# A transformer block on one core: the output projection done as three split products, its sums transposed back

## Chip, cores and metric

The kernel runs on 1 core of one Trainium2 chip. The metric is the device time in microseconds. Before the change the median of 3 runs is 757.2 us (757.11 to 757.91).

## What is computed

16 sequences of 256 rows with 128 features go through attention and a mixture of experts. Cut to what matters here:

```python
x = L0_attn_x                                   # (16, 256, 128)
xn = layernorm(x)
q, k, v = per head (16 heads of 64): xn @ Wq[h], xn @ Wk[h], xn @ Wv[h]
attn = softmax(causal(q @ k.T / 8))
heads = concat over h of attn @ v               # (256, 1024) for each sequence
y = xn + heads @ Wo                             # Wo: (1024, 128)
x1 = x + layernorm(layernorm(y, 1e-3) * gamma + beta)
# router: top 2 of 8 experts for each row, gelu(row @ w1[e]) @ w2[e], gated sum
out = x1 + layernorm(experts(layernorm(x1)))
```

The change concerns `heads @ Wo` and what reads its result.

## The kernel before

The five engines run programs of their own, written out by hand in order, and meet at semaphores. The attention is a loop over 16 batches (one sequence each, two tiles of 128 rows), each of `STEPS` = 4 steps; a step takes two pairs of heads. Below, step 1 to step 4 stand for u = 0 to 3. Several batches are under way at once: while batch b is in the steps, batch b-1 has its output sums normalised and batch b-2 goes through the router. After the 16 batches, 39 tiles of 256 rows go through the experts (lines 691 to 725), and at the end the two results of each row are summed and normalised.

One step on PE (line 480): the projection of one pair's q and k, `product3` twice (lines 384 to 395, six products of 256 columns on operands of type F32R, high and low parts; the low by low product is left out); the transposes of an earlier pair's probabilities (`p_transpose`, lines 439 to 448, the late rows into bank PT1O first); `w_o` for one pair (line 431); the second pair's projection, `p_transpose` and `w_o`; a third of the values' projection (`v_proj`, line 397); attention times values for two pairs (`pv_two`, line 427, into PT1O); the scores of the next two pairs and their masks (lines 402 to 416).

`w_o` takes the head sums `hT` (features on the partitions, in plain F32) as the stationary operand and `wo_sb` as the moving one, once for each of the two row tiles, and adds up over the 8 pairs in bank A:

```python
last = mm(A[:, t * D:(t + 1) * D], hT[:, par, t * P:(t + 1) * P], wo_sb[:, c, :], ...)
```

The result has the rows on the partitions. `hT` is made by one ACT copy out of PT1O at each step (`o_copy`, line 1278), which counts `o_sb`; PE waits on `o_sb` before it writes PT1O again with `p_transpose`, and before `w_o`.

One step on DVE (line 811): the maxima of the first pair's scores (lines 777 and 778); the copy of the late transposes `pT1` (line 794); `normalise_pair` of an earlier pair (lines 784, 786, 788), whose end, `nrm`, PE's second `p_transpose` waits for; the maxima of the second pair, again the copy and, behind some work of other batches, `normalise_pair`. The work of other batches has fixed places. For batch b-1 these are: `attended` (line 1042, adds `xn` to bank A) and `attention_stats` in step 2, `first_norm` (z1) and `second_stats` in step 3, `finish` (z3) in step 4. POOL makes the inverse roots between them, `z2 = z1 * gamma + beta` after `first_norm`, and `x1` after `finish`. For batch b-2, parts 0 to 6 of `router` are spread over the steps, with `dispatch` of batch b-3 at the end of step 1.

One step on ACT (line 1313): the copies of q and k, the exponentials, the copies of the transposes, `v_copy` (line 1273) out of bank M, and `o_copy`. In step 2 PE transposes the next batch's rows into bank M (`x_transpose`, line 375), for which it waits for `v_copy`, and only then come the scores.

After the last batch, `last_pairs` and `last_sums` (lines 578 to 605 for PE, 891 for DVE) finish the attention between the first products of the experts.

## Time and profile before

| | |
|---|---|
| median of 3 runs | 757.2 us |
| profiled execution, its own time | 757.12 us |
| its span on the core | 755.3 us |
| mean granted TensorE clock | 0.981 of full speed |
| busy share of the span | PE 93%, weight load 79%, DVE 75%, ACT 69%, POOL 37% |
| chain that ended last, by engine | PE 51%, DVE 24%, ACT 14%, POOL 2%, DMA 2%, issue and the queues the rest |
| the part before the experts | from 0 to some 570 us |

A busy time counts an instruction from start to end, and neighbours overlap: a matmul that the profile gives 0.28 us may be followed by the next after 0.12 us. What an instruction takes of its engine is the distance to the next start, and it is this that the chain of waits shows. A busy share is a mean over stretches that have different limits.

### The profile page before, as it was taken

The numbers are of one execution on the slowest core, as the hardware profiler recorded it, in microseconds if no ns is written. First come the engines' busy times: TensorE is split into PE (matmuls) and PEld (weight loads), VectorE is DVE, ScalarE is ACT, GpSimd is POOL, SyncE is SP. The second block draws the span as 40 slices with busy tenths as digits, with TensorE's granted clock in tenths as the row PEclk, the third lists the DMA queues.
The fourth block names the chain that finished last, engine by engine and source line by source line (L and its number), as shares of the span: only waits on it lengthen the run. The fifth ranks groups of instructions, "written<-read, shape, count | busy, mean of one in ns | idle before, by whom it ended". The sixth has DMA issues, their size and how long they took to land.

```text
span 755.3 us, 17697 instructions
## 1 busy us (share of the span) xinstructions
PE 700.0 (93%) x5954; PEld 596.4 (79%) x5955; DVE 564.9 (75%) x1914; ACT 524.5 (69%) x1687; POOL 277.5 (37%) x388
## 2 busy tenths in 40 slices
PE   4899999999999999999999999999989897999954
PEld 3688877788888888888888888888879797999921
DVE  5568888889897988888797988888896673444216
ACT  4776877877787777887787778887774563555505
POOL 3022534232323233232323232232314676655535
PEclk9999999999999999999999999999999998999978
DMA  8620000000000000000000000000020233222155
GB/s 184 205 40 8 9 8 16 17 27 10 23 8 23 8 23 16 17 23 15 22 8 23 8 23 13 19 23 9 16 66 30 73 111 97 76 78 79 45 175 173
DMA packets 43701, 34.88 MB, mean 46 GB/s; under 512 B 10624, under 2 KB 40320, under 8 KB 43616
## 3 DMA queue, kind: packets, MB, share of 16 engines
q1 hardware_dynamic: 37984, 23.81, 12.0%
q0 software_dynamic: 4544, 9.45, 3.5%
q8 instruction: 47, 0.77, 0.4%
q10 hardware_dynamic: 1088, 0.54, 0.3%
q14 instruction: 38, 0.31, 0.1%
HBM read 20.22 MB, written 13.56 MB: 45 GB/s over the span
## 4 chain that ended last, share of the span: by engine, by line
PE 51%; DVE 24%; ACT 14%; issue 4%; DMA 2%; DVEq 2%; POOL 2%; SPq 0%; POOLq 0%; ACTq 0%
PE M L684 8%; PE SC L406 6%; PE PT1O L423 6%; DVE prob L786 5%; ACT prob L1266 4%; PE SC L414 3%; DVE prob L788 3%; ACT prob L1260 3%; PE M L385 3%; DVE nmax L778 3%; PE PT1O L442 3%; PE SC L409 3%; ACT qk L1255 3%; PE M L387 2%; PE M L386 2%
## 5 line engine op out<-in xcount | busy, mean ns | idle before, releaser
L1255 ACT ACTIVATE qk<-M 128x512 f32<-128x512 f32 x127 | 76.1, 599 | 96.2 <-PE M L387 96.2
L1266 ACT ACTIVATE prob<-SC,nmax 128x256 f32<-128x256 f32 x256 | 123.5, 482 | 0.0
L423 PE MATMUL PT1O<-pT,v_sb 128*64 128x256 f32 (+1 forms) x1024 | 97.7, 333 | 0.7 <-ACT pT L1271 0.7
L423 PEld LDWEIGHTS PT1O<-pT,v_sb 128*64 128x64 f32 x1024 | 63.6, 137 | 42.5 <-issue 21.7
L1536 POOL DMA_INDIRECT expert_rows<-v_sb,got x78 | 77.1, 989 | 52.1 <-ACT v_sb L1410 33.9
L1260 ACT ACTIVATE prob<-SC,nmax 128x128 f32<-128x128 f32 x256 | 93.3, 370 | 3.6 <-DVE nmax L778 3.6
L786 DVE TENSOR_TENSOR prob<-prob,rden 128x512 f32<-128x512 f32 x128 | 90.1, 704 | 4.5 <-DVE rden L784 0.2
L1525 POOL DMA_INDIRECT sent_rows<-rec,slot x64 | 67.1, 1049 | 56.9 <-DVE slot L1030 37.9
L778 DVE TENSOR_REDUCE nmax<-SC 128x2 f32<-128x512 f32 x128 | 87.1, 680 | 0.0
L385 PE MATMUL M<-xt_hi,wqk_hi 128*128 128x256 f32 x254 | 82.6, 325 | 3.3 <-DVE xt_lo L772 2.4
L406 PE MATMUL SC<-qk 64*128 64x256 f32 x512 | 83.6, 403 | 0.6 <-ACT prob L1266 0.6
L777 DVE TENSOR_REDUCE nmax<-SC 128x2 f32<-128x256 f32 x128 | 53.4, 417 | 38.2 <-PE SC L414 38.0
L1271 ACT ACTIVATE pT<-PT 128x512 f32<-128x512 f32 x128 | 76.3, 596 | 3.8 <-PE PT L447 3.0
L684 PE MATMUL M<-w_sb,hidT 128*128 x624 | 78.0, 279 | 0.9 <-ACT v_sb L1410 0.9
L434 PE MATMUL A<-wo_sb,hT 128*128 128x128 f32 x512 | 78.2, 276 | 0.0
L684 PEld LDWEIGHTS M<-w_sb,hidT 128*128 128x128 f32 x624 | 74.5, 196 | 1.2 <-issue 1.1
L387 PE MATMUL M<-xt_hi,wqk_lo 128*128 128x256 f32 x254 | 72.0, 283 | 0.0
L386 PE MATMUL M<-xt_lo,wqk_hi 128*128 128x256 f32 x254 | 71.9, 283 | 0.0
L434 PEld LDWEIGHTS A<-wo_sb,hT 128*128 128x128 f32 x512 | 67.5, 193 | 0.0
L1410 ACT ACTIVATE v_sb<-M,got 128x128 f32<-128x128 f32 x78 | 24.4, 363 | 57.1 <-PE M L684 55.6
L442 PE MATMUL PT1O<-ident,prob 128*128 128x128 f32 x256 | 52.8, 288 | 11.3 <-DVE prob L788 8.0
L447 PE MATMUL PT<-ident,prob 128*128 128x128 f32 x256 | 63.2, 274 | 0.0
(186 smaller groups left out, 1789.3 us busy)
## 6 DMA issues: line engine op xcount, KB each, us to landing
got<-sent_rows SPq DMA_DIRECT2D x39, 132.0 KB, 2.3
w_in<-expert_rows SPq DMA_DIRECT2D x16, 256.0 KB, 3.6
x_in<-L_attn_x SPq DMA_DIRECT2D x16, 128.0 KB, 2.1
w_in<-L_ffn_w SPq DMA_DIRECT2D x1, 2048.0 KB, 12.0
x_res<-L_attn_x SPq DMA_DIRECT2D x16, 128.0 KB, 2.1
w_sb<-L_ffn_w SPq DMA_DIRECT2D x8, 256.0 KB, 4.4
out<-y_out SPq DMA_DIRECT2D x8, 256.0 KB, 2.1
sent_rows<-pad_rec SPq DMA_DIRECT2D x11, 132.0 KB, 4.2
```

Source lines behind the costliest of these rows:

```text
L385: mm(dst, a_hi, b_hi, start=start, stop=False, skip_group_check=True)
L386: mm(dst, a_hi, b_lo, start=False, stop=False, skip_group_check=True)
L387: return mm(dst, a_lo, b_hi, start=False, stop=True, skip_group_check=True)
L406: mm(SC[par][:, k, LATE_Q], qk[r, par, 0, P:S], qk[r, par, 1, :], start=True, stop=False, skip_group_check=True)
L423: last = mm(PT1O[k * E:(k + 1) * E, cols], v_sb[:, t, h * E:(h + 1) * E], src[:, par, k, :], start=(t == 0), stop=(t == 1), skip_group_che ...
L434: last = mm(A[:, t * D:(t + 1) * D], hT[:, par, t * P:(t + 1) * P], wo_sb[:, c, :], start=(c == 0 and t == 0), stop=(c == NP - 1), skip_gr ...
L684: last = mm(out_bank[:, t * D:(t + 1) * D], hidT[:, s, c, t * P:(t + 1) * P], w2_e[:, c * D:(c + 1) * D], start=(t == 0 and c == 0), stop= ...
L778: v.tensor_reduce(nmax[:, par, 0, :], SC[par][:, :, LATE_Q], AX_X, ALU.max, negate=True).then_inc(mx, 1)
L786: v.tensor_tensor(prob[:, slot, :, 1:3, :], prob[:, slot, :, 1:3, :], rden[:, par, 0, :].unsqueeze(2).unsqueeze(3).broadcast_to([P, 2, 2, ...
L1255: a.activation(qk[:, p % 2], src[:].rearrange("p (i s) -> p i s", i=2), ACT.Copy).then_inc(qk_sb, 1)
L1260: return a.activation(prob[:, slot, k, 0, :], SC[par][:, k, EARLY_Q], ACT.Exp, bias=nmax[:, par, 1, k:k + 1], accum_out=den[:, par, 1, k:k ...
L1266: return a.activation(prob[:, slot, k, 1:3, :].rearrange("p n t -> p (n t)"), SC[par][:, k, LATE_Q], ACT.Exp, bias=nmax[:, par, 0, k:k + 1 ...
```

## The change

- The output weights are split at the start into `wo_hi` and `wo_lo` (POOL, two instructions of 1024 columns behind `pad_ids(0)`), and PE's first `w_o` waits for them.
- `o_copy` writes `hT_hi` (type F32R), and DVE makes `hT_lo` = PT1O - `hT_hi` in a new instruction `o_low`, 128x512, at the start of every step, in front of the maxima. It is now `o_low` that counts `o_sb`.
- `w_o` is one `product3` for a pair: three products of 256 columns, weights stationary, head sums moving. Bank A holds the sums transposed.
- In step 2 ACT copies them to `att_t` (`sums_copy`, in front of `v_copy`), and PE transposes them back into bank A (`sums_transpose`, in front of `x_transpose`).
- `attended` reads them from there and moves from step 2 to the start of step 3. `attention_stats` moves from the end of step 2 to the middle of step 3, `first_norm` from the middle of step 3 to its end, `second_stats` from the end of step 3 to the middle of step 4, `finish` from the middle of step 4 to its end. `xn` gets a third buffer for this.
- To make room, `hidT`, the experts' hidden rows, shares the memory of `wqk_in`, and `y_out` that of `prob`.

```diff
-        xn = [sb(f"xn{n}", [P, T, D]) for n in range(2)]
+        xn = [sb(f"xn{n}", [P, T, D]) for n in range(3)]
...
             def w_o(c):
                 par = c % 2
-                for t in range(T):
-                    last = mm(A[:, t * D:(t + 1) * D], hT[:, par, t * P:(t + 1) * P], wo_sb[:, c, :],
-                              start=(c == 0 and t == 0), stop=(c == NP - 1), skip_group_check=True)
+                last = product3(A[:, 0:S], wo_hi[:, c, :], wo_lo[:, c, :], hT_hi[:, par, :], hT_lo[:, par, :],
+                                start=(c == 0))
...
+            def sums_transpose(b):
+
+                pe.wait_ge(sem("att_t"), b + 1)
+                for t in range(T):
+                    last = nc.tensor.transpose(A[:, t * D:(t + 1) * D], att_t[:, t * P:(t + 1) * P], ident[:])
+                last.then_inc(sem("sums_mm"), 1)
...
+                if k == 2:
+                    pe.wait_ge(sem("wo_ok"), 1)
...
+                if u == 1 and there(b, 1):
+                    sums_transpose(b - 1)
...
             def in_front_of_down(n):
+                if n == 1:
+                    sums_transpose(B - 1)
...
+            def o_low(k):
+                dve.wait_ge(sem("o_hi"), k)
+                v.tensor_tensor(hT_lo[:].rearrange("c n (t p) -> c n t p", t=T),
+                                PT1O[:].rearrange("c (n p t) -> c n t p", n=2, t=T),
+                                hT_hi[:].bitcast(F32).rearrange("c n (t p) -> c n t p", t=T), ALU.subtract).then_inc(o_sb, 1)
...
+                if u == 2 and there(b, 1):
+                    attended(b - 1)
+                if k >= 2:
+                    o_low(k - 1)
                 maxima(p)
...
                 if u == 1:
-                    if there(b, 1):
-                        attended(b - 1)
...
                 if u == 2:
                     if there(b, 1):
-                        first_norm(b - 1)
+                        attention_stats(b - 1)
...
                 if u == 3:
                     if there(b, 1):
-                        finish(b - 1)
+                        second_stats(b - 1)
...
-                if u == 1:
-                    if there(b, 1):
-                        attention_stats(b - 1)
                 if u == 2:
...
                     if there(b, 1):
-                        second_stats(b - 1)
+                        first_norm(b - 1)
                 if u == 3:
                     if there(b, -2):
                         x_stats(b + 2)
+                    if there(b, 1):
+                        finish(b - 1)
...
                 expert_weights(1, w1_at[1])
                 split_rows(1, 1, M[:, ROWS:2 * ROWS])
+                o_low(STEPS * B - 1)
                 normalise_pair(end - 1)
                 pT1_copy(end - 2)
...
                 pT1_copy(end - 1)
+                o_low(STEPS * B)
...
             def o_copy(k):
                 act.wait_ge(pv_mm, k)
-                a.activation(hT[:].rearrange("c n (t p) -> c n t p", t=T), PT1O[:].rearrange("c (n p t) -> c n t p", n=2, t=T),
-                             ACT.Copy).then_inc(o_sb, 1)
+                a.activation(hT_hi[:].rearrange("c n (t p) -> c n t p", t=T), PT1O[:].rearrange("c (n p t) -> c n t p", n=2, t=T),
+                             ACT.Copy).then_inc(sem("o_hi"), 1)
+
+            def sums_copy(b):
+                act.wait_ge(sem("wo_mm"), b + 1)
+                if there(b, 1) and there(b, -1):
+                    act.wait_ge(sem("lg_done"), b)
+                a.activation(att_t[:], A[:, 0:S], ACT.Copy).then_inc(sem("att_t"), 1)
...
+                if u == 1 and there(b, 1):
+                    sums_copy(b - 1)
                 turn = v_turn(b, u)
...
+            pool.wait_ge(sem("wo_ld"), 16)
+            q.tensor_copy(wo_hi[:], wo_sb[:]).then_inc(sem("wo_h"), 1)
+            pool.wait_ge(sem("wo_h"), 1)
+            q.tensor_tensor(wo_lo[:], wo_sb[:], wo_hi[:].bitcast(F32), ALU.subtract).then_inc(sem("wo_ok"), 1)
```

Line numbers of the changed kernel differ from those before: its maxima are lines 795 and 796, its `normalise_pair` 802 to 806, its normalisations 773.

The first place is DVE at the seam of steps 3 and 4 in a steady batch, from the last part of `normalise_pair` to the next maxima. Before:

```order
L788 TENSOR_TENSOR prob<-prob,rden 128x2x128
L770 CAST xt_hi<-xt_st 128x256 [waits xt_st,v_mm]
L772 TENSOR_TENSOR xt_lo<-xt_st,xt_hi 128x256 [waits xt_h]
L745 BN_STATS stat_z<-z 128x6 [waits z2_done]
L745 BN_STATS stat_z<-z 128x6
L750 BN_AGGR mv_z<-stat_z 128x2 x2
L777 TENSOR_REDUCE nmax<-SC 128x2 [waits s_mm]
L778 TENSOR_REDUCE nmax<-SC 128x2
```

Now:

```order
L806 TENSOR_TENSOR prob<-prob,rden 128x2x128
L788 CAST xt_hi<-xt_st 128x256 [waits xt_st,v_mm]
L790 TENSOR_TENSOR xt_lo<-xt_st,xt_hi 128x256 [waits xt_h]
L773 TENSOR_SCALAR z<-att,mv_a,rstd_a 128x128 [waits rstd_a]
L773 TENSOR_SCALAR z<-att,mv_a,rstd_a 128x128
L831 TENSOR_TENSOR hT_lo<-PT1O,hT_hi 128x512 [waits o_hi]
L795 TENSOR_REDUCE nmax<-SC 128x2 [waits s_mm]
L796 TENSOR_REDUCE nmax<-SC 128x2
```

The statistics of z are gone from here, the normalisation to z1 (two instructions) is here in their place, and in front of the maxima stands the new subtraction with its wait on `o_hi`.

The second place is DVE in the middle of step 4, behind the second maxima and the copy `pT1`. Before:

```order
L778 TENSOR_REDUCE nmax<-SC 128x2
L794 COPY pT<-PT1O 128x256 [waits t1_mm]
L755 TENSOR_SCALAR z<-z,mv_z,rstd_z 128x128 [waits rstd_z]
L755 TENSOR_SCALAR z<-z,mv_z,rstd_z 128x128
L1003 CAST topf<-topi 128x16
L1006 TENSOR_TENSOR sel<-iota_e,topf 128x16 x2
L1008 TENSOR_TENSOR sel_bf<-sel 128x16
```

Now:

```order
L796 TENSOR_REDUCE nmax<-SC 128x2
L812 COPY pT<-PT1O 128x256 [waits t1_mm]
L763 BN_STATS stat_z<-z 128x6 [waits z2_done]
L763 BN_STATS stat_z<-z 128x6
L768 BN_AGGR mv_z<-stat_z 128x2 x2
L1032 CAST topf<-topi 128x16
L1035 TENSOR_TENSOR sel<-iota_e,topf 128x16 x2
L1037 TENSOR_TENSOR sel_bf<-sel 128x16
```

The two instructions that made z3 have left for the end of the step, and the statistics of z stand here.

The third place is PE at the end of step 2, between `pv_two` and the scores. Before:

```order
L423 MATMUL PT1O<-pT,v_sb 64x256 x2
L423 MATMUL PT1O<-pT,v_sb 64x128 x2
L378 MATMUL M<-ident,xn 128x128 [waits xn_done,v_done]
L378 MATMUL M<-ident,xn 128x128
L406 MATMUL SC<-qk 128x256 [waits exp_done,qk_sb]
```

Now:

```order
L429 MATMUL PT1O<-pT,v_sb 64x256 x2
L429 MATMUL PT1O<-pT,v_sb 64x128 x2
L448 MATMUL A<-ident,att_t 128x128 [waits att_t]
L448 MATMUL A<-ident,att_t 128x128
L384 MATMUL M<-ident,xn 128x128 [waits xn_done,v_done]
L384 MATMUL M<-ident,xn 128x128
L412 MATMUL SC<-qk 128x256 [waits exp_done,qk_sb]
```

Two transposes that wait for ACT's copy `att_t` have come in front of those of the next batch's rows.

## Rows read from the trace of the kernel before

**Rows 1.** Windows, one steady batch: busy us (x) of PE, PEld, DVE, ACT, POOL; PEclk; DMA

```profile
305.00:339.00 34.00, 33.51 (x301) 28.05 (x297) 29.38 (x103) 26.79 (x94) 10.61 (x15) 1.00 0.06 17
```

**Rows 2.** Chain of waits, two steps in the middle: start us, us, engine, tile, line

```profile
305.24 0.44 PE M L378 x2
...
324.85 0.23 PE PT1O L442 x2
...
326.34 0.35 DVE prob L788
...
326.73 0.44 PE PT1O L442 x2
...
327.61 0.45 PE A L434 x4
...
331.92 0.54 PE SC L414 x4
...
332.68 0.12 PE M L385
...
333.43 0.60 ACT qk L1255
...
338.79 0.49 ACT v_sb L1275
...
339.33 0.44 PE M L378 x2
```

**Rows 3.** Timeline of DVE, same stretch: start, us, what, [idle before <-releaser]

```profile
322.82 0.48 DVE L745 BATCH_NORM_STATS2 stat_x<-x_in 128x6 f32<-128x128 f32 x2
...
323.54 0.14 DVE L1014 COPY rec<-top 128x2 f32<-128x2 f32 x1
...
323.95 0.42 DVE L777 TENSOR_REDUCE nmax<-SC 128x2 f32<-128x256 f32 x1
...
325.10 0.43 DVE L794 COPY pT<-PT1O 128x256 f32<-128x256 f32 x1
...
326.59 0.42 DVE L777 TENSOR_REDUCE nmax<-SC 128x2 f32<-128x256 f32 x1
...
327.52 0.42 DVE L794 COPY pT<-PT1O 128x256 f32<-128x256 f32 x1
...
331.90 0.17 DVE L1030 CAST slot<-slot_f 128x4 int32<-128x4 f32 x1
332.28 0.42 DVE L777 TENSOR_REDUCE nmax<-SC 128x2 f32<-128x256 f32 x1 [0.21 <-PE SC L414]
...
333.69 0.42 DVE L794 COPY pT<-PT1O 128x256 f32<-128x256 f32 x1 [0.39 <-PE PT1O L442]
```

**Rows 4.** Line 1180 on DVE, durations in ns: min/median/max, first and last start

```profile
L1180 DVE TENSOR_TENSOR wv_hi<-PT,wv_hi x37: 424/425/425, 571.8 to 711.3; 128x256 fp32r<-128x256 f32 x37
```

**Rows 5.** Timeline of ACT, end of the second step of a batch

```profile
305.77 0.41 ACT L1250 ACTIVATE xt_st<-M 128x256 f32<-128x256 f32 x1
306.06 0.20 ACT L1289 ACTIVATE ex<-lg 128x16 f32<-128x16 f32 x1
```

**Rows 6.** Lines 994 and 1003 on DVE as in Rows 4; POOL timeline

```profile
L994 DVE TENSOR_TENSOR pr<-ex,rrs x16: 174/448/454, 105.0 to 609.7; 128x16 f32<-128x16 f32 x16
L1003 DVE CAST topf<-topi x16: 175/750/753, 114.3 to 611.7; 128x16 f32<-128x16 uint32 x16
320.41 0.73 POOL L1512 TENSOR_TENSOR x<-x_res,z 128x256 f32<-128x256 f32 x1 [3.18 <-DVE z L755]
```

**Rows 7.** Timelines of PE and DVE, behind the last step of attention

```profile
564.77 1.05 PE L434 MATMUL A<-wo_sb,hT 128*128 128x128 f32 x8
...
564.92 0.17 DVE L784 RECIPROCAL rden<-den 128x4 f32<-128x4 f32 x1
```

**Rows 8.** Timeline of PE, first batch; chain of waits near 560 us

```profile
30.05 0.44 PE L378 MATMUL M<-ident,xn 128*128 128x128 f32 x2 [0.92 <-ACT v_sb L1275]
...
559.77 0.85 PE A L434 x4
```

More of the change, by code:

```diff
@@ L80, in sandwich_kernel @@
         wo_sb = sb("wo_sb", [P, NP, D])
+        wo_hi = sb("wo_hi", [P, NP, D], F32R)
+        wo_lo = sb("wo_lo", [P, NP, D], F32R)
         w1_in = sb("w1_in", [P, NE, F])
@@ L111, in sandwich_kernel @@
         pT1 = sb("pT1", [P, 2, 2, P])
-        hT = sb("hT", [P, 2, S])
+        hT_hi = sb("hT_hi", [P, 2, S], F32R)
+        hT_lo = sb("hT_lo", [P, 2, S], F32R)
+        att_t = sb("att_t", [P, S])
         shift = sb("shift", [P, 2, GT])
@@ L177, in sandwich_kernel @@
         w1_e = wqk_hi[:].rearrange("p i c -> p (i c)").rearrange("p (s i f) -> p s i f", s=2, i=2)
-        hidT = sb("hidT", [P, 2, NF, ROWS])
+        hidT = wqk_in[:].rearrange("p i c -> p (i c)").rearrange("p (s c r) -> p s c r", s=2, c=NF)
         yo = v_sb[:].rearrange("p t c -> p (t c)")[:, 0:RING * ROWS].rearrange("p (k t d) -> p k t d", k=RING, t=2)
@@ L183, in sandwich_kernel @@
         zn = hidT[:, 0].rearrange("p c r -> p (c r)").rearrange("p (s k d) -> p s k d", s=2, k=GT)
-        y_out = sb("y_out", [P, 2, GT, D])
+        y_out = prob[:].rearrange("p s k n t -> p (s k n t)")[:, 0:2 * GT * D].rearrange("p (s k d) -> p s k d", s=2, k=GT)
         SC = [ctx.enter_context(nc.psum_tensor(f"SC{n}", [P, 2, 512], F32)) for n in range(2)]
@@ L377, in x_transpose @@
                 for t in range(T):
-                    last = nc.tensor.transpose(M[:, t * P:(t + 1) * P], xn[b % 2][:, t, :], ident[:])
+                    last = nc.tensor.transpose(M[:, t * P:(t + 1) * P], xn[b % 3][:, t, :], ident[:])
                 last.then_inc(sem("xt_mm"), 1)
@@ L477, in _ @@
             pe.wait_ge(sem("wv_ok"), 1)
-            pe.wait_ge(sem("wo_ld"), 16)
             def step(b, u):
@@ L809, in _ @@
             v.tensor_tensor(wv_lo[:], wv_in[:], wv_hi[:].bitcast(F32), ALU.subtract).then_inc(sem("wv_ok"), 1)
+            def o_low(k):
[3 more added lines that the diff above has]
+                                hT_hi[:].bitcast(F32).rearrange("c n (t p) -> c n t p", t=T), ALU.subtract).then_inc(o_sb, 1)
             def step(b, u):
-                p = 2 * (STEPS * b + u)
+                k = STEPS * b + u
+                p = 2 * k
                 first = p == 0
+                if u == 2 and there(b, 1):
+                    attended(b - 1)
+                if k >= 2:
+                    o_low(k - 1)
                 maxima(p)
@@ L1037, in x_normalise @@
                 dve.wait_ge(sem("rstd_x"), b + 1)
-                if b >= 2:
-                    dve.wait_ge(sem("att_done"), b - 1)
-                normalise("x", xn[b % 2], x_in, T).then_inc(sem("xn_done"), 1)
+                if b >= 3:
+                    dve.wait_ge(sem("att_done"), b - 2)
+                normalise("x", xn[b % 3], x_in, T).then_inc(sem("xn_done"), 1)
             def attended(b):
-                dve.wait_ge(sem("wo_mm"), b + 1)
+                dve.wait_ge(sem("sums_mm"), b + 1)
                 if there(b, 1) and there(b, -1):
                     dve.wait_ge(sem("logit_mm"), b)
-                v.tensor_tensor(att[:], xn[b % 2][:], A[:, 0:T * D].rearrange("p (t d) -> p t d", t=T), ALU.add)\
+                v.tensor_tensor(att[:], xn[b % 3][:], A[:, 0:T * D].rearrange("p (t d) -> p t d", t=T), ALU.add)\
                     .then_inc(sem("att_done"), 1)
@@ L1428, in _ @@
                     gated(n, k, it)
+                    if n == 0:
+                        sums_copy(B - 1)
             with act.Fori(EARLY // RING, TILES // RING) as it:
```

## The prediction

> **What bounds the kernel now.** I read the windows first, then the chain of waits over one batch, then the timelines of DVE, ACT and PE over the same stretch. A batch takes 34.09 us, from one transposing of the next rows to the following (305.24 to 339.33 [rows 2]). In a steady batch PE is busy 33.5 of 34 us and DVE 29.4 [rows 1], so PE looks like the bound and DVE like an engine with 4.6 us to spare. The chain says something narrower. In steps 1 and 4 it passes from PE's late transposes (324.85 [rows 2]) to DVE's copy `pT1` (325.10 [rows 3]), over the normalisation (its end at 326.34 + 0.35) back to PE (326.73), and stays on PE until the masks (331.92) [rows 2]. In step 2 it runs on ACT without a gap from the copy of q and k (333.43) to `v_copy` (338.79), and PE's transposes of the next rows wait for that (339.33) [rows 2]. In step 3 it runs mostly on DVE. What decides is thus not how much DVE idles but where. At the seam of steps 4 and 1 the maxima start at 323.95 with no idle in front of them. A pair of maxima takes 0.93 us (326.59 to 327.52), so they end at 324.88, and the copy behind them starts at 325.10: 0.22 us of room. At the seam of 1 and 2 there is 0.21 us of idle in front of the maxima (332.28), which end at 333.21, and the copy starts at 333.69: 0.48 more [rows 3]. From 3 to 4 there is none. The rest of DVE's idle time lies in step 2, while ACT works.
>
> **What PE gains.** A `w_o` takes 0.45 us before, one F32R product of 256 columns 0.12 [rows 2], so three of them 0.36: 0.09 less, for 128 calls 11.5 us. The two transposes back take 0.23 (as the pair at 324.85 [rows 2]), 16 times 3.7. PE's own work falls by 7.8 us. Little of it reaches the end: the first `w_o` of a step is done while DVE normalises, the second is on the chain in steps 1 and 4 only, and there DVE will be later than PE.
>
> **What ACT adds.** `sums_copy` is a copy of 128x256 out of PSUM. The one of the same size at 305.77 is followed at 306.06 [rows 5]: 0.29 us. It stands in front of `v_copy` in step 2, where ACT is the chain, so it counts in full. The transposes back on PE fall into the wait for `v_copy`.
>
> **What DVE adds.** `o_low`, 128x512, PSUM minus SBUF, has no equal in the trace. The nearest is line 1180, half its size, 424 ns [rows 4]; its distance to the next start is about 0.34. The pair of maxima reads 768 elements of PSUM in 0.93 us [rows 3], which for 512 makes 0.62. I take 0.62; the ends are 0.34 and 0.69 (the time that the normalisation takes for its 512 elements).
>
> By the Trainium skill (VectorE: DVE Perf Modes, the errata section), a DVE instruction that reads PSUM takes 120 cycles more than its elements at 0.96 GHz, an estimate of 0.66 us here; the sum would be 1.6 us higher.
>
> DVE's order is the second half of the matter. `attended` and `attention_stats` leave step 2, where DVE has time. `attended` is at the start of step 3 still in that time. `attention_stats` is not: it takes the place of `first_norm`, that of `second_stats`, that of `finish`, and `finish` goes to the end of step 4. So the stretch from the first maxima of step 3 to the first copy `pT1` of the next step 2 holds one set of statistics more, 0.72 us (322.82 to 323.54 [rows 3]), and three `o_low`. The fourth, in front of step 3's maxima, waits only for ACT's copy, which is there before the masks: free.
>
> Walk along that stretch: it is DVE alone, work after work, once the room is used up. Added: 3 x 0.62 + 0.72 = 2.58 us. Room used up: 0.22 + 0.21 + 0.48 = 0.91 [rows 3]. That leaves 1.67, and with ACT's 0.29 a batch takes 1.96 us more.
>
> Against that stands a relief. Line 994 takes 448 ns in the loop and 174 at least, line 1003 750 and 175 [rows 6]. Line 994 runs while POOL makes z2, and line 1003 starts together with POOL's x1 at 320.41 [rows 6]: the two engines get in each other's way on SBUF operands. Line 1180, with one operand in PSUM, never varies (424 to 425 ns [rows 4]). In the changed order z2 falls under `o_low` and the maxima, which read PSUM, so line 994 gets back 0.27 us. x1 moves away from line 1003, which gets back up to 0.57, but now starts beside the small copies of `router` part 6; I take half, 0.28. So a batch costs 1.96 - 0.55 = 1.41 us.
>
> The stretch is full from batch 2's step 3 (the router's parts are there from then on) to batch 15's step 2: 13 times, 18.3 us. In batches 0 and 1 DVE has room, PE's 0.09 in some steps and ACT's 0.29 once cancel: 0.
>
> **The end of the attention.** In batch 15 step 2 has PE on the chain, so 0.23 - 0.09 = 0.14. `o_low` in front of step 4's maxima, less the relief of line 994: 0.35. In `last_pairs` PE reaches the double `w_o` at 564.77, while DVE begins its normalisation at 564.92 [rows 7]; the new `o_low` stands in front of that normalisation and PE now waits for it. That is 0.62 for `o_low` itself, the 0.15 between the two starts, and about as much again as `o_low` (an estimate) for `finish`, which has moved in front of it: 1.4 us, less 0.18 for the faster `w_o`. Together 1.7 us. `sums_transpose` in front of the second tile and the last `o_low` have the first tile's stores beside them: nothing. The split of the weights on POOL lies in the first step, where POOL idles, and PE's first `w_o` comes in the third: nothing; if it were late, that `w_o` would wait a few us once. The shared memory of `hidT` and `y_out` moves no instruction.
>
> **Sum.** 18.3 + 0 + 1.7 = 20.0 us on the profiled execution's 757.12, which is 0.1 below the median of the runs: 777 us.
>
> **Rivals.**
> *PE sets the time (faster).* If DVE had 0.62 us of room at each seam, PE's 7.8 us less would show: 749 us. For it speaks PE's busy share, 33.5 of 34 [rows 1]. Against it: the maxima at 323.95 have no idle in front of them and 0.22 behind [rows 3]. It decides if an `o_low` takes under about 0.25 us. Chance 0.04.
> *Only ACT's copy counts.* If the moved statistics and the subtractions find room after all (router parts cheaper in the new order), 15 x 0.29 less some of PE's gain and plus the 1.7 us of the end: 761 us. Against it again the seam without idle. Chance 0.07.
> *POOL and DVE collide more.* After the change POOL's two instructions for z2 begin as DVE passes into step 4, its inverse root runs beside line 1006, and x1 beside part 6 of the router. If no relief comes and one more instruction is held for as long as line 1003 is (0.57), a batch takes 1.96 + 0.3 to 0.57: 757 + 13 x 2.4 + 2 = 790 us. Chance 0.13.
> By the Trainium skill (SBUF: State Buffer, the section on the two separate sides), the pair of ports that DVE and GpSimd share goes whole to whichever starts first, for all of its instruction, and a DVE instruction contends if it has two SBUF inputs or runs in a two-port mode; by this rule the router's copies would lose the full length of x1, which is this rival. The durations of lines 994 and 1003 agree with it.
> *The clock falls.* PE now waits about 2 us more in each batch. A TensorE at half clock takes 0.85 us for a `w_o` at 559.77, against 0.45 [rows 2, 8]. If that came once a batch for some 4 us, 13 x 2 = 26 more: 803 us. Against it: the waits are split over three steps, and after one of 0.92 us in the first batch the transposes still take their 0.44 us [rows 2, 8], as at 339.33. The granted clock in the window is 1.00 [rows 1]. Chance 0.05.
>
> **How the numbers follow.** My forecast has 0.71. Its own bounds: `o_low` at 0.34 makes 39 x 0.28 = 11 less, 766; at 0.69, no relief, 777 + 3 + 7 = 787. The range 766 to 789 takes in nearly all of the forecast and the smaller half of the collisions; left out are 749, 761, 803 and the top of the collisions, some 0.2. A change of 0.2%, 1.5 us, is about what a measurement of this kernel can tell from none. Faster 0.04, same 0.02 (a lower case of the second rival), slower 0.94.
>
> **What would show it.** In the profile after: `o_low` 64 times with a mean near 0.69 us busy; DVE without idle from step 3 to step 2, its idle time gathered in front of the maxima of step 3; PE waiting for `nrm` or `o_sb` in steps 4 and 1, up to 0.7 us each; the batches 35.5 us long, where they were 34.09; the product in F32R at 0.12 us for each of three; the clock at 1.00. Wrong would be: idle time on DVE at the seams of steps 3, 4 and 1; PE's `w_o` products further apart than 0.12; a batch under 34.5 us.

## The result, and the profile after

| | before | after |
|---|---|---|
| median of 4 runs each | 757.33 us | 779.3 us (777.88 to 780.77) |
| ratio after to before, 95% interval | | 1.0296 (1.0271 to 1.0321) |
| profiled execution, its own time | 757.12 us | 780.77 us |
| its span on the core | 755.3 us | 779.0 us |
| mean granted clock of TensorE | 0.981 | 0.980 |
| busy share: PE, DVE, ACT | 93%, 75%, 69% | 90%, 76%, 68% |
| chain that ended last: PE, DVE, ACT, issue | 51, 24, 14, 4% | 38, 34, 14, 6% |

The change costs 22.0 us, 2.9%. The forecast was 20 us more (777, range 766 to 789). The profiled execution is the longest of the four, so its span shows 23.7. PE's busy time is as good as unchanged (700.0 us before, 701.4 after); DVE took over part of PE's share of the chain.

The same stretch as in [rows 1], windows view, busy us of PE, PEld, DVE, ACT, POOL, then PEclk:

```profile
305.00:339.00 34.00, 32.04 (x279) 26.14 (x275) 30.19 (x98) 26.23 (x93) 10.52 (x15) 1.00 0.06 17
```

Less PE, more DVE, in a stretch that no longer holds a whole batch. Two successive transposes of the next rows give its length (timeline of PE, as the first and last of [rows 2]):

```profile
312.86 0.44 PE L384 MATMUL M<-ident,xn 128*128 128x128 f32 x2
...
348.46 0.44 PE L384 MATMUL M<-ident,xn 128*128 128x128 f32 x2
```

That is 35.60 us, 34.09 before. The forecast was 35.5. Now the timeline of DVE, from the start of step 3 over the seams to steps 4 and 1 (columns as in [rows 3]):

```profile
312.84 0.42 DVE L1075 TENSOR_TENSOR att<-xn,A 128x256 f32<-128x256 f32 x1 [0.55 <-PE A L448]
313.32 0.69 DVE L831 TENSOR_TENSOR hT_lo<-PT1O,hT_hi 128x512 fp32r<-128x512 f32 x1
315.17 0.42 DVE L795 TENSOR_REDUCE nmax<-SC 128x2 f32<-128x256 f32 x1 [1.15 <-PE SC L420]
...
319.07 0.48 DVE L763 BATCH_NORM_STATS2 stat_a<-att 128x6 f32<-128x128 f32 x2
...
319.78 0.14 DVE L1019 TENSOR_REDUCE rsum<-ex 128x2 f32<-128x16 f32 x1
...
323.44 0.68 DVE L831 TENSOR_TENSOR hT_lo<-PT1O,hT_hi 128x512 fp32r<-128x512 f32 x1
324.04 0.41 DVE L795 TENSOR_REDUCE nmax<-SC 128x2 f32<-128x256 f32 x1
...
331.83 0.16 DVE L1043 COPY rec<-top 128x2 f32<-128x2 f32 x1
331.90 0.71 DVE L1044 CAST rec<-ids 128x2 int32<-128x2 f32 x1
332.52 0.68 DVE L831 TENSOR_TENSOR hT_lo<-PT1O,hT_hi 128x512 fp32r<-128x512 f32 x1
333.12 0.41 DVE L795 TENSOR_REDUCE nmax<-SC 128x2 f32<-128x256 f32 x1
```

`o_low` takes 0.60 us of DVE (323.44 to 324.04; 0.62 forecast). Nothing is idle in front of the maxima at 324.04 and 333.12; the idle time stands mostly in front of step 3's `attended` (0.55) and its maxima (1.15). Outside the lines shown there is 0.25 us in step 1, where DVE waits for POOL's inverse root as it did before the change, and 0.41 in step 2, where it waits for PE's products of the router. `attention_stats` (319.07 to 319.78, 0.71) stands in the full stretch. So far it is the picture of the prediction. The rows of the three lines that POOL can hold, of the DVE line groups in ns (min/median/max), as [rows 6]:

```profile
L831 DVE TENSOR_TENSOR hT_lo<-PT1O,hT_hi x64: 672/684/693, 31.0 to 593.0; 128x512 fp32r<-128x512 f32 x64
...
L1023 DVE TENSOR_TENSOR pr<-ex,rrs x16: 174/207/214, 106.0 to 633.2; 128x16 f32<-128x16 f32 x16
...
L1032 DVE CAST topf<-topi x16: 175/212/742, 114.9 to 635.2; 128x16 f32<-128x16 uint32 x16
...
L1044 DVE CAST rec<-ids x32: 157/184/728, 118.0 to 638.3; 128x2 int32<-128x2 f32 x32
```

Line 994 (now 1023) fell from 448 to 207 ns and line 1003 (now 1032) from 750 to 212; but one of each pair of line 1044 now takes 0.71 us, beside POOL's x1. The collision with x1 moved by one place and did not go.

How late the changed kernel runs, place by place in the two profiled executions:

| place | before | after | later by |
|---|---|---|---|
| next rows of batch 4 transposed | 134.01 | 134.92 | 0.91 |
| the same, eleven batches on | 509.96 | 526.79 | 16.83 |
| `pv_two` in batch 15, step 2 | 543.22 | 561.48 | 18.26 |
| `pv_two`, step 3 | 551.35 | 569.90 | 18.55 |
| `pv_two`, step 4 | 561.41 | 581.50 | 20.09 |
| `pv_two` in `last_pairs` | 569.41 | 590.84 | 21.43 |
| last two `w_o` start | 572.92 | 596.84 | 23.92 |
| end of the span | 755.3 | 779.0 | 23.7 |

Eleven steady batches cost 15.92, 1.45 each. The end of the attention costs 23.92 - 18.26 = 5.7, where the prediction had 1.7. There PE's timeline of the changed kernel reads:

```profile
576.17 0.41 PE L454 MATMUL PT1O<-ident,prob 128*128 128x128 f32 x2 [2.70 <-issue]
...
581.50 2.62 PE L429 MATMUL PT1O<-pT,v_sb 128*64 128x256 f32 x16
...
590.84 1.52 PE L429 MATMUL PT1O<-pT,v_sb 128*64 128x256 f32 x16 [0.69 <-ACT pT L1300]
...
596.84 0.36 PE L391 MATMUL A<-hT_hi,wo_hi 128*128 128x256 f32 x1 [2.32 <-DVE before L987]
...
601.03 1.95 PE L702 MATMUL M<-w_sb,wqk_in 128*128 x16
```

and DVE's:

```profile
593.04 0.69 DVE L831 TENSOR_TENSOR hT_lo<-PT1O,hT_hi 128x512 fp32r<-128x512 f32 x1 [2.86 <-ACT hT_hi L1309]
595.05 0.43 DVE L1201 CAST wqk_hi<-w_hi 128x512 fp32r x1 [1.32 <-issue]
...
596.52 0.17 DVE L987 COPY before<-A 128x24 f32<-128x24 f32 x1
```

The last `w_o` write bank A, so they also wait for DVE to have copied batch 13's counts out of it. That copy stands in DVE's order behind the last `o_low`, the reading of the next tile's expert number (1.32 us of issue) and that tile's splits. Before the change DVE did all of these while ACT copied the head sums; now it waits 2.86 us for ACT first.

### The profile page after: what moved, and what is told of

Its sections match the earlier page's. It is cut to its first block, busy times and chain, and to the rows that moved or that the text cites. A ratio compares the mean times of both kernels' runs of the same rounds, so it can differ in the third digit from the quotient of the medians.

```text
span 779.0 us, 17600 instructions
## 1 busy us (share of the span) xinstructions
PE 701.4 (90%) x5858; PEld 588.8 (76%) x5859; DVE 595.2 (76%) x1978; ACT 530.7 (68%) x1703; POOL 285.1 (37%) x390
## 4 chain that ended last, share of the span: by engine, by line
PE 38%; DVE 34%; ACT 14%; issue 6%; DVEq 3%; POOL 2%; DMA 2%; POOLq 0%; SPq 0%; ACTq 0%
PE M L702 6%; DVE prob L804 6%; PE SC L412 5%; DVE nmax L796 4%; ACT prob L1295 4%; PE PT1O L429 4%; DVE prob L806 3%; ACT prob L1289 3%; PE SC L420 3%; DVE nmax L795 2%; DVE hT_lo L831 2%; DVE pT L812 2%; ACT qk L1284 2%; ACT pT L1300 2%; PE M L391 2%
## 5 line engine op out<-in xcount | busy, mean ns | idle before, releaser
L1569 POOL DMA_INDIRECT sent_rows<-rec,slot x64 | 70.1, 1095 | 55.6 <-DVE slot L1059 37.4
L391 PE MATMUL M<-xt_hi,wqk_hi 128*128 128x256 f32 x254 | 77.4, 305 | 2.2 <-ACT xt_st L1279 1.3
L702 PE MATMUL M<-w_sb,wqk_in 128*128 x624 | 77.9, 279 | 1.1 <-ACT v_sb L1447 1.1
L702 PEld LDWEIGHTS M<-w_sb,wqk_in 128*128 128x128 f32 x624 | 74.4, 195 | 1.3 <-issue 1.3
L454 PEld LDWEIGHTS PT1O<-ident,prob 128*128 128x128 f32 x256 | 26.7, 141 | 50.8 <-DVE prob L806 33.1
L458 PE MATMUL PT<-ident,prob 128*128 128x128 f32 x256 | 63.2, 274 | 0.0
L459 PE MATMUL PT<-ident,prob 128*128 128x128 f32 x256 | 63.2, 274 | 0.0
```

The source lines that it names most:

```text
L391: mm(dst, a_hi, b_hi, start=start, stop=False, skip_group_check=True)
L454: last = nc.tensor.transpose(PT1O[:, par * S + k * P:par * S + (k + 1) * P], prob[:, slot, k, 2, :], ident[:])
L702: last = mm(out_bank[:, t * D:(t + 1) * D], hidT[:, s, c, t * P:(t + 1) * P], w2_e[:, c * D:(c + 1) * D], start=(t == 0 and c == 0), stop= ...
```

## The experiments

A period is the mean over the eleven steady batches, from the transposes of the next rows near 134 us to those eleven batches on; by the same count it is 34.18 us before the change and 35.62 after. Ratios are against the kernel before on the same chip. From chip to chip the median of that kernel lies between 755.7 and 757.3 us, so a difference of two medians is uncertain by some 1.5 us; ratios and periods are the better measure.

| run | from | median us | ratio (95%) | period us |
|---|---|---|---|---|
| no o_low | after | 762.34 | 1.0065 (1.0050 to 1.0080) | 34.51 |
| two products | after | 777.16 | 1.0266 (1.0237 to 1.0294) | 35.50 |
| no way back | after | 775.41 | 1.0226 (1.0190 to 1.0261) | 35.35 |
| statistics early | after | 770.80 | 1.0189 (1.0163 to 1.0215) | 35.01 |
| counts ahead | after | 778.18 | 1.0285 (1.0270 to 1.0300) | 35.64 |
| last o_low late | after | 775.55 | 1.0250 (1.0235 to 1.0265) | 35.64 |
| norm early | before | 752.27 | 0.9943 (0.9928 to 0.9957) | 34.11 |
| no o_low, statistics early | after | 755.13 | 0.9976 (0.9963 to 0.9990) | 34.22 |
| before plus o_low | before | 770.42 | 1.0195 (1.0173 to 1.0218) | 34.97 |
| o_low twice | after | 805.27 | 1.0657 (1.0638 to 1.0676) | 37.40 |
| statistics early, last o_low late | after | 767.15 | 1.0142 (1.0121 to 1.0164) | 34.99 |
| the same, records first | after | 761.65 | 1.0062 (1.0037 to 1.0087) | 34.46 |

**Is it o_low, and is it DVE?** Four runs ask it: first, the changed kernel without it:

```diff
-                if k >= 2:
-                    o_low(k - 1)
                 maxima(p)
...
-                last = product3(A[:, 0:S], wo_hi[:, c, :], wo_lo[:, c, :], hT_hi[:, par, :], hT_lo[:, par, :],
-                                start=(c == 0))
+                last = product2(A[:, 0:S], wo_hi[:, c, :], wo_lo[:, c, :], hT_hi[:, par, :], start=(c == 0))
```

> The changed kernel without o_low: VectorE's subtraction and the product with hT_lo are gone, and ScalarE's copy counts o_sb itself as before the change. It leaves out the low part of the head sums. VectorE's order sets the batch (my theory): three subtractions of 0.60 us on the path go, 1.8 us for each of 13 batches, so the period falls from 35.6 to about 33.8 us, no longer than before the change, and the kernel takes 779.3 - 13 x 1.8 = 756 us, some 2 us less if the end of the attention recovers too; window of one batch: VectorE some 28 us busy. Rival, TensorE's own work sets it: 128 products of 0.12 us less, 779.3 - 15.4 = 764 us. Rival, ScalarE's copy and the way back are what counts: about 777 us.

762.3 us: 17 less, and the period falls by 1.11 instead of 1.8 us. I had forgotten my own term: without `o_low` the seams' room comes back (0.91 us, [rows 3]). It is more than the 0.72 of the moved statistics, so by the prediction's terms only ACT's copy is left, 34.18 + 0.29 = 34.47; measured is 34.51. PE's timeline shows it waiting there still, and DVE idles longer in front of step 3's maxima:

```profile
329.01 0.44 PE L457 MATMUL PT1O<-ident,prob 128*128 128x128 f32 x2 [0.79 <-DVE prob L809]
```
```profile
309.61 0.42 DVE L798 TENSOR_REDUCE nmax<-SC 128x2 f32<-128x256 f32 x1 [1.90 <-PE SC L424]
```

This run takes DVE's work and PE's away together; the next takes PE's alone (the second half of the diff above, without the first).

> The changed kernel with o_low kept but the product with hT_lo left out, which takes 0.12 us of TensorE's work from each of 128 w_o calls and leaves VectorE and ScalarE as they are; it leaves out the low part of the head sums. If VectorE's order sets the batch: period unchanged at 35.6 us, TensorE only waits longer, 778 to 779.5 us. Rival, TensorE's work sets it: 128 x 0.12 = 15.4 us less, 764 us.

777.2 us: 2.1 less for 15.4 us of work taken away, and the period 0.12 us shorter for eight `w_o` of 0.12 less each. PE's lost work is answered by longer waits (0.57 where the same place had 0.47):

```profile
324.88 0.44 PE L457 MATMUL PT1O<-ident,prob 128*128 128x128 f32 x2 [0.57 <-DVE prob L809]
```

PE does not set the batch after the change. The remaining fall of the first run is DVE's. Now DVE's work alone, put on the kernel before:

```diff
+                if k >= 2:
+                    o_low(k - 1)
                 maxima(p)
...
-                             ACT.Copy).then_inc(o_sb, 1)
+                             ACT.Copy).then_inc(sem("o_hi"), 1)
```

> The kernel before with one instruction per step added: o_low on VectorE at the start of the step, as in the change, writing a tile that nobody reads; o_sb is counted by it and so TensorE waits for it as in the change. All else is as before the change. Taken alone, as the prediction's terms have it: three o_low of 0.62 us on the path less the 0.91 us of room give 0.95 us for each of 13 batches, 12.3 us, and about 3 us at the end of the attention: 757 + 15 = 772 us, period 35.05 us. Rival, the whole 0.60 us of all four steps counts: 2.4 us per batch, 788 us. Rival, TensorE sets the time and hides it: 757 us.

770.4 us, 14.8 above the 755.7 of the kernel before on the same chip (15 forecast). The period, from PE's timeline:

```profile
310.63 0.44 PE L379 MATMUL M<-ident,xn 128*128 128x128 f32 x2
...
345.56 0.44 PE L379 MATMUL M<-ident,xn 128*128 128x128 f32 x2
```

34.93 here, 34.97 in the mean, so 0.79 more than before. Three times 0.60 less 0.79 leaves 1.01 us of room, read as 0.91 from [rows 3]. With the room used up, the price must be the full 0.60 each; so I doubled it:

```diff
             def o_low(k):
                 dve.wait_ge(sem("o_hi"), k)
+                v.tensor_tensor(spare[:].rearrange("c n (t p) -> c n t p", t=T),
+                                PT1O[:].rearrange("c (n p t) -> c n t p", n=2, t=T),
+                                hT_hi[:].bitcast(F32).rearrange("c n (t p) -> c n t p", t=T), ALU.subtract)
```

> The changed kernel with a second subtraction of the same size (128x512 from PSUM, 0.60 us) ahead of each o_low, into a spare tile. In steps 4, 1 and the start of that stretch VectorE has no idle time, so if its order sets the batch three of the four are paid in full: 1.8 us for each of 13 batches, period 37.4 us, 779.3 + 23.4 + about 1 at the end = 804 us; the fourth, in step 3, is taken up by the 1.15 us of idle time. Rival, the stretch has room left or ScalarE and TensorE pace it: less than half of it, under 791 us. Rival, all four count: 811 us.

805.3 us, 26 more, and the period 1.78 longer: three of the four subtractions in full. The one in step 3 fell into idle time, which shrank from 1.15 to 0.55 us, by one subtraction:

```profile
325.87 0.69 DVE L832 TENSOR_TENSOR spare<-PT1O,hT_hi 128x512 fp32r<-128x512 f32 x1
326.47 0.68 DVE L835 TENSOR_TENSOR hT_lo<-PT1O,hT_hi 128x512 fp32r<-128x512 f32 x1
327.71 0.42 DVE L796 TENSOR_REDUCE nmax<-SC 128x2 f32<-128x256 f32 x1 [0.55 <-PE SC L421]
```

**The way back** (no `sums_copy`, no `sums_transpose`):

```diff
-                if u == 1 and there(b, 1):
-                    sums_transpose(b - 1)
...
-                if u == 1 and there(b, 1):
-                    sums_copy(b - 1)
...
-                dve.wait_ge(sem("sums_mm"), b + 1)
+                dve.wait_ge(sem("wo_mm"), b + 1)
```

> The changed kernel without the way back: no sums_copy on ScalarE, no transposes of the sums on TensorE, attended waits for the last w_o and adds the sums as they lie. It leaves out the turning back of the sums, so they are added transposed. As the prediction has it, ScalarE's copy costs 0.29 us on the path of step 2 in each batch: 14 x 0.29 = 4 us less, 775 us. Rival, the way back is covered, since step 3's maxima wait 1.15 us for the scores anyway: 779 us. Rival, the wait of attended (0.55 us) is paid too: 14 x 0.84 = 12 us less, 767 us.

775.4 us, the period 0.27 shorter: ACT's copy counts, as its term of 0.29 said, and the wait of `attended` does not. The run takes PE's two transposes away too, but they are not what counts: the next rows' transposes start 0.68 us behind the start of `v_copy` here (309.67 to 310.35) and 0.69 in the changed kernel (312.17 to 312.86), where `sums_copy` puts `v_copy` off by 0.26 (311.91 to 312.17).

**The moved statistics.** The order of step 3 changed so that they use the idle time:

```diff
                 if k >= 2:
                     o_low(k - 1)
+                if u == 2 and there(b, 1):
+                    attention_stats(b - 1)
                 maxima(p)
...
                 if u == 2:
-                    if there(b, 1):
-                        attention_stats(b - 1)
```

> The changed kernel with attention_stats moved from the middle of step 3 to its start, behind attended and o_low, where VectorE's trace shows 1.15 us of idle time in front of the maxima; nothing is left out. If VectorE's full stretch from step 3's first maxima on sets the batch: 0.71 us less in each of 13 batches, 779.3 - 9.2 = 770 us, period 34.9 us, idle in front of step 3's maxima 0.4 us. Rival, the stretch is paced by TensorE and VectorE's order only follows: 779 us, and the 0.7 us show up as idle time of VectorE in step 4 or 1.

770.8 us, 8.5 less, the period 0.61 shorter. The statistics fill the gap and the maxima follow:

```profile
310.65 0.47 DVE L763 BATCH_NORM_STATS2 stat_a<-att 128x6 f32<-128x128 f32 x2
311.55 0.25 DVE L768 BATCH_NORM_AGGREGATE mv_a<-stat_a 128x2 f32<-128x6 f32 x2 [0.42 <-issue]
311.88 0.42 DVE L795 TENSOR_REDUCE nmax<-SC 128x2 f32<-128x256 f32 x1
```

From the start of `o_low` to the maxima it is 1.84 us (from 310.04), and 1.85 without this edit (313.32 to 315.17), so they cost nothing there. 0.71 us left the stretch and 0.61 came back; the other 0.10 I did not trace.

**The end of the attention**, in two forms. First only the counts' copy moved:

```diff
                 pT1_copy(end - 1)
+                counts_copy(B - 3, True)
                 o_low(STEPS * B)
```

> The changed kernel with one copy moved at the end of the attention: the counts of batch 13 (128x24, 0.17 us) are copied ahead of the last o_low instead of behind it and the next tile's weights; nothing is left out. In the trace of the changed kernel TensorE waited 2.32 us for that copy in front of its last sums (to 596.84), though o_low had ended at 593.64. If this order of VectorE costs the end of the attention: the last w_o starts some 3 us earlier, at about 593.8 from the same start; the product behind it still wants the splits that end at 596.5, so 1 to 2 us less in all, 777.5 to 778.5 us. Rival, the experts' stage takes it back, since its own chain starts from the splits: 779.3 us.

778.2 us. From the last batch's transposes to the last `w_o` it took 67.5 us (527.84 to 595.31) instead of 70.0: 2.6 earlier there, but in the median 1.1 us, which the intervals hardly tell from nothing. Then the last `o_low` moved instead:

```diff
                 pT1_copy(end - 1)
-                o_low(STEPS * B)
...
                 if n == 0:
                     counts_copy(B - 3, True)
+                    o_low(STEPS * B)
                     dispatch(B - 3)
```

> The changed kernel with the last o_low moved behind the next tile's weights, their splits and the counts, so that VectorE does these while it would wait 2.86 us for ScalarE's copy of the head sums; nothing is left out. If VectorE's order at the end of the attention is what the prediction had too low (1.7 us foreseen, some 5 us measured at the last w_o): the last w_o starts some 2 us earlier and the splits end some 2.5 us earlier too, 2 to 3 us less in all, 776.5 us; a run of low clock in 580 to 600 us may go with it. Rival, the experts' stage takes it back: 779.3 us.

775.6 us. DVE's and PE's timelines:

```profile
592.39 0.43 DVE L1201 CAST wqk_hi<-w_hi 128x512 fp32r x1 [1.59 <-issue]
...
594.19 0.17 DVE L987 COPY before<-A 128x24 f32<-128x24 f32 x1
594.27 0.68 DVE L831 TENSOR_TENSOR hT_lo<-PT1O,hT_hi 128x512 fp32r<-128x512 f32 x1
```
```profile
591.46 1.52 PE L429 MATMUL PT1O<-pT,v_sb 128*64 128x256 f32 x16 [0.69 <-ACT pT L1300]
...
595.01 0.38 PE L391 MATMUL A<-hT_hi,wo_hi 128*128 128x256 f32 x1
...
597.69 1.95 PE L702 MATMUL M<-w_sb,wqk_in 128*128 x16
```

The reading of the expert's number and the splits lie in the wait for ACT again, and from the last `pv_two` to the second tile's `down` it takes 6.23 us where the changed kernel took 10.19 (590.84 to 601.03). Some 1.1 us of these 4.0 are TensorE's clock: the twelve products behind the last `w_o` take 1.42 us here (595.83 to 597.25, 0.12 apart) and 2.56 in the changed kernel (597.79 to 600.35, 0.21 apart). With only the counts moved the same way took 7.80 us (591.88 to 599.68), since behind the last `w_o` the next product waited 1.49 us for the splits (597.75). So by this stretch the counts alone are 2.4 of the 4.0 us; by the medians they are 1.1 of 3.8. A single profile can't settle the shares: in this one `last_pairs` took 11.20 us (580.26 to 591.46) against 9.34, with the granted clock at 0.60 from 587 to 590.

**Do the repairs add up?** Statistics early and the last o_low late in one kernel:

> The changed kernel with the edits of e4_stats_early and e5b_low_late together, nothing left out: the best version of the change from these runs. They touch different stretches, so the savings should add up: 8.5 + 3.5 us less than the change, 779.3 - 12 = 767 us, still 1.3% above the kernel before. Rival, the end's saving is lost since another wait of the end is the last one: 770 us.

767.2 us, 12.1 less than the change, where the two alone gave 8.5 and 3.8. On top of it the collision with x1, which the profile after had shown moved by one place:

```diff
-                    if there(b, 1):
-                        finish(b - 1)
                     if there(b, 2) and not is_last(b):
                         router(b - 2, 6)
+                    if there(b, 1):
+                        finish(b - 1)
```

> The kernel e9_stats_and_end (767.15 us) with one more order changed on VectorE at the end of step 4: the four small copies into the records (L1043, L1044) go ahead of finish and not behind it, nothing left out. Behind finish the last of them runs beside GpSimd's add of x1 and takes 0.71 us where the other of its line takes 0.16; ahead of finish GpSimd is idle, and what then runs beside the add is o_low, which another trace shows beside GpSimd's z2 at its usual 0.60 us. If it is the collision that costs: 0.55 us less in each of 13 batches, period 34.45 us, 767.15 - 7 = 760 us. Rival, o_low or the first maxima are held instead by the add: unchanged, 767 us. Rival, TensorE or the chain of one step paces the batch already at 35.0 us: less than 0.2 us per batch, 765 us.

761.7 us, the period 0.53 shorter. Timeline of DVE, its line group, and the timeline of POOL:

```profile
325.75 0.16 DVE L1044 CAST rec<-ids 128x2 int32<-128x2 f32 x1
325.82 0.60 DVE L773 TENSOR_SCALAR z<-z,mv_z,rstd_z 128x128 f32<-128x128 f32 x2
326.33 0.68 DVE L831 TENSOR_TENSOR hT_lo<-PT1O,hT_hi 128x512 fp32r<-128x512 f32 x1
```
```profile
L1044 DVE CAST rec<-ids x32: 160/164/301, 118.1 to 620.8; 128x2 int32<-128x2 f32 x32
```
```profile
326.50 0.73 POOL L1556 TENSOR_TENSOR x<-x_res,z 128x256 f32<-128x256 f32 x1 [2.57 <-DVE z L773]
```

The add starts 0.17 us after `o_low` and neither holds the other. In these rows POOL holds a small DVE operation on SBUF for its whole length, and does not hold a subtraction with one operand in PSUM. This is the change at its best here, still 0.6% above the kernel before. It still has one collision more than that kernel, in the last batch (see the part on the end of the attention).

**A version that beats both?** Two candidates. One is the changed kernel without `o_low` and with the statistics early (the edits of the first and the fifth diff):

> The changed kernel without o_low and without the product with hT_lo (as in the run e1_no_low: the low part of the head sums is left out), and with attention_stats at the start of step 3 (as in e4_stats_early). If the costs add up, since all of them lie in one full stretch of VectorE: e1's 762.3 less 0.58 us in each of 13 batches (what e4 measured per batch), 754.8 us, period 33.9 us and so below the kernel before; the two-product form takes 0.12 + 0.12 us where the form before took 0.45. Rival, e1 is already paced by TensorE or ScalarE's copy, since its period is 34.4 to 34.7 and not 33.8 us: 761 to 762 us.

755.1 us, a quarter of a per cent under the kernel before, and it leaves out the low part of the head sums. The time was forecast at 754.8, but that it came out is partly luck: the period is 34.22 us and not 33.9, 0.29 less than without the early statistics where 0.58 was forecast, and not below the 34.18 of the kernel before. So the rival, that other engines pace the batch already, had half of it; where the rest of the gain lies I did not trace. The other is the kernel before with one normalisation earlier:

```diff
                 first = p == 0
+                if u == 2 and there(b, 1):
+                    first_norm(b - 1)
                 maxima(p)
...
                 if u == 2:
-                    if there(b, 1):
-                        first_norm(b - 1)
```

> The kernel before with one thing moved: first_norm goes from the middle of step 3 to its start, ahead of the first maxima, where VectorE's trace shows 1.38 us of idle time; GpSimd then multiplies z2 before VectorE's small router operations instead of beside them (L994 at 0.45 us and not 0.17). Nothing is left out. If VectorE's stretch takes part in setting the batch even before the change: up to 0.51 + 0.25 us less in each of 13 batches, 757 - 10 = 747 us; but TensorE is busy 33.5 of 34 us there, so I take 0.3 us per batch, 753 us. Rival, TensorE alone set the batch before the change: 757 us.

752.3 us, the fastest kernel of this study, and not for the reason I gave. POOL's z2 now comes early and line 994 keeps its short time (line group of DVE, timeline of PE):

```profile
L994 DVE TENSOR_TENSOR pr<-ex,rrs x16: 175/175/177, 105.4 to 606.6; 128x16 f32<-128x16 f32 x16
```
```profile
98.39 0.44 PE L378 MATMUL M<-ident,xn 128*128 128x128 f32 x2
...
133.40 0.44 PE L378 MATMUL M<-ident,xn 128*128 128x128 f32 x2
```

but the steady batches stayed where they were, 34.11 us against 34.18. DVE did not set them before the change, so time given back to it there is worth almost nothing. The batch from 97.85 to 134.01, in which POOL also splits the first layer's weights, fell from 36.16 to 35.01: beside these splits several DVE operations last longer than usual, and in the new order fewer of them do. At the last transposes the kernel is 1.33 us ahead (509.96 to 508.63). The other large part lies in batch 15. From `pv_two` of step 3 to that of step 4 it takes 8.34 us (550.27 to 558.61) where the kernel before took 10.06 (551.35 to 561.41): PE waits 1.68 us for DVE's normalisation instead of 2.47, and the granted clock is 1.00 in 551 to 559, where the kernel before had 0.84 in 552 to 562. That the shorter wait is what kept the clock up is likely, but not shown. At `pv_two` of `last_pairs` the kernel is 3.19 us ahead (569.41 to 566.22), at the end 4.0 (span 755.3 to 751.3).

## Why the prediction held, and where it did not

**The bound.** That DVE's order from step 3 to step 2 would take the place of PE is shown: a second `o_low` costs three of its four parts in full, PE's work removed alone gives 2.1 of 15.4 us.

**o_low.** 0.62 forecast, 0.60 measured; the nearest row by kind (the maxima, PSUM in, by elements) gave the right value. The room of 0.91 us, read from one idle time and two distances in [rows 3], came out as 1.01 when `o_low` was put on the kernel before. By the Trainium skill (VectorE: DVE Perf Modes, the errata section) the estimate was 0.66; the trace has 0.68 as the busy time of one and 0.60 as the distance to the next, and it is the distance that the chain pays.

**PE's own work.** A `w_o` was to take 0.09 us less and PE 7.8 us less in all; nothing came of it. The prediction priced all three products at 0.12. In the changed kernel the first of them is followed only after 0.20, so that a `w_o` takes 0.44 us (349.30 to 349.74) against 0.45, and from the late transposes to the next projection it is 1.01 us in both kernels (324.69 to 325.70 before, 348.73 to 349.74 after). The term enters the sum only with 0.09 and 0.18, so the error did not show; the rival of 749 us rested on it.

**The batch.** 1.41 forecast, 1.44 measured (35.62 - 34.18). Part by part: `o_low` against the room 0.95, measured 0.79; the moved statistics 0.72, measured 0.61; ACT's copy 0.29, measured 0.27; line 994 minus 0.27, in its row minus 0.24. Measured parts: 0.79 + 0.61 + 0.27 - 0.24 = 1.43. The parts were taken from different starting points, so that they close so well is partly luck.

**The mis-sized relief.** Two terms of the sum failed, this one and the end of the attention. "x1 moves away from line 1003 [...] I take half, 0.28": it gave nothing. Line 1003 won 0.54 and line 1044 lost 0.55. The rival had this mechanism, but as an addition to the lost relief. By the Trainium skill (SBUF — State Buffer, the section on the two separate sides) the ports that DVE and GpSimd share go whole to one of them; line 1044 at 0.71 beside x1 and 0.16 without agrees. Moving it was worth 0.53 us per batch. Other terms were somewhat too large, which hid this one.

**The batches together.** 18.3 forecast, 18.26 measured at step 2 of batch 15, but not by the same parts. The prediction counted batch 2 to 3 among the thirteen at 1.41 us; it cost 0.11 (36.16 before, 36.27 after), and the traces show why. POOL splits the first layer's weights in that batch. Before the change DVE's line 788 lasts 0.95 us twice (107.08 and 117.01; usually 0.42), line 772 once 0.90 (usually 0.43) and line 1008 once 0.65 (usually 0.18), all beside these splits, 2.0 us in sum. In the changed order only one of the four is long (line 806 at 111.91, 0.95), so 1.5 us come back. The run with `o_low` alone on the kernel before has all four long, and there this batch costs 1.19 (98.42 to 135.77). The first two batches, forecast at nothing, were 0.80 later, most of it (0.49) at the transposes in batch 0, whose time differs from run to run by more than that (30.05 to 31.41 us in kernels with the same start). The twelve others cost 1.45 each. The three misses, -1.30, +0.80 and +0.4, cancel, which is luck.

**The end of the attention.** Here the prediction failed most: 1.7 forecast, 5.7 measured. "`sums_transpose` in front of the second tile and the last `o_low` have the first tile's stores beside them: nothing" was wrong by 2.5 us. I asked who waits for `o_low` (PE's last `w_o`) and not what is queued behind it on DVE: the counts' copy, for which the same `w_o` wait.

The other error is the way from step 3 to step 4 of batch 15, 0.35 forecast and 1.54 measured. The prediction had "In the changed order z2 falls under `o_low` and the maxima, which read PSUM". In the last batch it does not: no splits of next rows stand there, and part 5 of the router comes directly behind `first_norm`, in front of `o_low`. So lines 1032 and 1035 run beside POOL's two instructions for z2. DVE's timeline after and before, and POOL's after:

```profile
573.04 0.74 DVE L1032 CAST topf<-topi 128x16 f32<-128x16 uint32 x1
573.86 0.81 DVE L1035 TENSOR_TENSOR sel<-iota_e,topf 128x16 f32<-128x16 f32 x2
...
576.00 0.40 DVE L795 TENSOR_REDUCE nmax<-SC 128x2 f32<-128x256 f32 x1
```
```profile
554.67 0.21 DVE L1003 CAST topf<-topi 128x16 f32<-128x16 uint32 x1
554.95 0.28 DVE L1006 TENSOR_TENSOR sel<-iota_e,topf 128x16 f32<-128x16 f32 x2
...
555.96 0.41 DVE L777 TENSOR_REDUCE nmax<-SC 128x2 f32<-128x256 f32 x1
```
```profile
573.03 0.73 POOL L1547 TENSOR_TENSOR z<-z,gamma_t 128x256 f32<-128x256 f32 x1 [1.99 <-DVE z L773]
573.84 0.72 POOL L1549 TENSOR_TENSOR z<-z,beta_t 128x256 f32<-128x256 f32 x1
```

The two lines last 1.06 us longer in sum. From `pv_two` of step 3 to these maxima it is 4.61 us before (551.35 to 555.96) and 6.10 after (569.90 to 576.00), 1.49 more. The kernel before with `o_low` alone has 5.21 there (563.38 to 568.59), the changed kernel without `o_low` 5.63 (557.51 to 563.14): `o_low` costs 0.60 alone and the new order 1.02 alone, together a little more than the 1.49. TensorE's clock is not the cause. It is at the lower of its levels there (the products of a `w_o` stand 0.21 apart at 576.78, 0.12 in the batches), but it was before the change too (granted 0.84 in 552 to 562, 0.78 in 570 to 582.5 after), and from the maxima to `pv_two` of step 4 both kernels take the same, 5.45 and 5.50 us.

The third part, `last_pairs` up to its `pv_two`, was forecast at 1.4 - 0.18 and took 1.34: right. Moving the last `o_low` gave back 3.8 us (779.3 to 775.55); in the one stretch where the two profiles can be laid side by side, 1.1 of 4.0 us was the clock.

**The rivals.** PE as the bound, ACT's copy alone, and a falling clock in the batches did not come; the granted clock is 1.00 in every window from 20 to 564 us. The extra collision came in half of its form in the steady batches, and in full in the last one.

## What to carry to other kernels

Count an engine's room at each seam of the loop, as an idle time or a distance in the timeline, and charge new work only past it; past it nearly every added microsecond counted here. When an instruction is inserted whose input comes late, list what stands behind it on its engine and who waits for that: at the end of a phase this was worth more than the instruction. Where a small SBUF operation is held beside a GpSimd tensor operation, try to put one that reads PSUM in its place; in these traces that one was not held. Look at the first and the last turn of a loop for themselves: where an operation is missing, its neighbours meet other partners.

## What the runs showed that I had not expected

- PE waited 2.32 us for a copy of 0.17 us (596.52) with whose data its sums have nothing to do; the two share bank A.
- The aggregate of the early statistics (311.55) starts only after 0.42 us of issue; at 319.62 in the changed kernel, the same pair of operations had no such gap. The runs do not explain it; in idle time it was free.
- The kernel before was itself 0.6% slower than it need be, by one normalisation that stood half a step late, and the 4 us came mostly from one early batch (1.15) and the last one (1.7 in one step), hardly from the steady ones.
- Not every POOL instruction holds DVE. Line 1035 takes its usual 0.28 us for its pair (328.88) beside POOL's inverse root of 0.70 (328.86), but 0.81 beside z2 in batch 15.
